# Seven PSUM banks in one pool, a bank named for each fill, and norms' gains and shifts applied behind the transpose

## Chip, cores and metric

The kernel runs on one core of one Trainium2 chip. The metric is the device time of one execution in microseconds, the median of several. All data are float32.

## The reference

The input x has 32 sequences of 64 rows by 256 features, and ctx has the same shape. Five attention blocks follow each other, here by the letters of the kernel's stages:

- n, a and d (first layer): x is normalised over a whole sequence, with a gain and a shift by row. Queries come from the normalised x, keys and values from ctx; 8 heads of 64 channels attend over the 256 feature positions, softmax(q k) v, then an output projection, a bias and x added.
- k and b (second layer): a = layernorm(ctx)*g + b; keys and values a @ Wk, a @ Wv; 16 heads of 16 over 64 keys; x + tanh(gate) * out.
- k and e (third layer): queries from x, keys and values from ctx and x together (128 keys), output projection and residual; then rmsnorm with a gain, `gelu(out @ w1 + b1) @ w2 + b2`, residual.
- c (fourth layer, first half): layernorm(x)*s1 + b1, self-attention with a mask, residual.
- k and f (fourth layer, second half): layernorm(x)*s2 + b2, attention over ctx, residual; layernorm(x)*s3 + b3, a gelu MLP, residual. The result is the output.

## The kernel before, in words

**Tiling.** Two sequences are one pair (128 rows), so there are 16 pairs. Each pair passes through the stages n, a, d, k, b, e, c, f. Every stage is written once for each engine as a Python generator (`pe_a`, `act_a`, `dve_a`, `pool_a` and so on); each `yield` ends a step.

**Order.** `weave` (called at the end of `build` for each engine) takes the strings of `ORDER`, one letter a step, and issues the steps of all pairs in that order. The order of work on every engine is thus fixed by these strings, and an engine that waits holds back all that is behind it on that engine. The strings of TensorE let stage a of later pairs run between b, e, c and f of earlier ones.

**Setup (stage s).** Before the pairs, gains and shifts of the norms are folded into weights: 80 matmuls with one column (L1135) multiply the weights by the norms' shifts, giving `fold` (used as biases), then VectorE multiplies eight weight blocks by the gains (L1196) and one by tanh(gate) (L1200), and four pairs of matmuls (L1146) turn value biases into rows, `row_bias`. The first transpose of stage d waits for `row_bias` (`setup["row"]`), and so do the projections of stage k (`ready`).

**Banks.** PSUM has eight banks of 512 columns here. Before the change four have fixed users in stages a and d: two for the scores and for the projections of queries and keys (`scores_bank`), one for transposed probabilities (`transposed_bank`), one for the attended values (`attended_bank`). All other stages share four (`banks`), taken in turn: `fill_places` gives fill number k the bank k % 4. `fill_bank` waits until the last reader of the bank's last fill has released it, `filled` says that it is full, `wait_fill` waits for that, `release` gives it back and `written` waits for the release.

**Stages a and d.** Of a pair there are 8 units (two sequences n, four pairs of heads j). `project(j)` (L441) fills both score banks, ScalarE and VectorE copy them out with a bias as q_a and k_a. `score` (L452) fills both banks with scores of two heads, and waits for the exponentials of the unit before. VectorE takes the maxima (L488), ScalarE the exponentials with their sums (L524), VectorE the reciprocals (L494), GpSimd multiplies (L538). `transpose` (L555) then fills `transposed_bank` for e = 0, waits for ScalarE's copy (L602, `pt0`), fills it for e = 1, and the next unit waits for VectorE's copy (L588, `pt1`). `attend` (L570) multiplies by the values.

**Norms of k, e, c, f.** VectorE computes statistics and the normalised rows, GpSimd the power -1/2, TensorE transposes (L607) and `act_copy` (L804) copies the transpose out in one 128x256 instruction; gains and shifts are in the weights already. ScalarE also runs Exp and Gelu; between the two a table is loaded.

**Residuals.** `pool_residual` (L764) adds a row of `row_bias` to the residual on GpSimd in every attention; in stage b that is a row made of the folded value bias.

## Time and profile before

| | us |
|---|---|
| median of 3 runs | 1444.21 (1443.49 to 1444.38) |
| the profiled execution | 1449.69 |
| its span, first to last instruction | 1447.9 |
| TensorE busy (matmul) | 1331.4 |
| VectorE, ScalarE, GpSimd busy | 1062.8, 812.6, 784.5 |
| mean granted TensorE clock | 0.963 |

The profiled execution is the one that all rows come from; the span is what its rows cover, and its own time is 1.8 us longer. A busy time counts instructions of that engine; the rest of the span is idle time, most of it waiting for another engine.

### The profile page before, as it was taken

The numbers are of one execution on the slowest core, as the hardware profiler recorded it, in microseconds if no ns is written. First come the engines' busy times: TensorE is split into PE (matmuls) and PEld (weight loads), VectorE is DVE, ScalarE is ACT, GpSimd is POOL, SyncE is SP. The second block draws the span as 40 slices with busy tenths as digits, with TensorE's granted clock in tenths as the row PEclk, the third lists the DMA queues.
The fourth block names the chain that finished last, engine by engine and source line by source line (L and its number), as shares of the span: only waits on it lengthen the run. The fifth ranks groups of instructions, "written<-read, shape, count | busy, mean of one in ns | idle before, by whom it ended". The sixth has DMA issues, their size and how long they took to land. (4 is left out here: it accounts for less than half of the span.)

```text
span 1447.9 us, 33972 instructions
## 1 busy us (share of the span) xinstructions
PE 1331.4 (92%) x12752; PEld 990.0 (68%) x12752; DVE 1062.8 (73%) x2251; ACT 812.6 (56%) x2043; POOL 784.5 (54%) x1072
## 2 busy tenths in 40 slices
PE   5898999999999999999999899999999999989685
PEld 4665666768686676867677676868686775757564
DVE  3458796887877878787877869697868778675742
ACT  2155557557575666665565656566566656654332
POOL 1145365565665665565565657474655656563631
PEclk8599999999999999999999999999999999999896
DMA  8000000000000000000000000000000000000000
GB/s 324 14 9 12 17 2 5 22 5 17 6 21 6 20 7 15 8 10 17 6 21 6 20 7 16 11 6 17 6 21 6 9 18 1 2 6 5 1 5 4
DMA packets 22815, 26.49 MB, mean 18 GB/s; under 512 B 9600, under 2 KB 21888, under 8 KB 22400
## 3 DMA queue, kind: packets, MB, share of 16 engines
q1 hardware_dynamic: 22656, 24.33, 5.2%
q8 instruction: 105, 1.72, 0.5%
q14 instruction: 54, 0.44, 0.1%
HBM read 22.22 MB, written 2.10 MB: 17 GB/s over the span
## 5 line engine op out<-in xcount | busy, mean ns | idle before, releaser
L538 POOL TENSOR_SCALAR p_a<-p_a,rec_a 128x256 f32<-128x256 f32 x512 | 249.4, 506 | 184.3 <-DVE rec_a L494 184.2
L524 ACT ACTIVATE p_a<-scores,nmax_a 128x256 f32<-128x256 f32 x512 | 236.3, 474 | 101.5 <-DVE nmax_a L488 96.8
L488 DVE TENSOR_REDUCE nmax_a<-scores 128x2 f32<-128x512 f32 x256 | 165.5, 680 | 50.4 <-PE scores L452 49.1
L555 PE MATMUL transposed<-ident,p_a 128*128 128x128 f32 x1024 | 166.1, 286 | 27.6 <-DVE p_a L588 9.8
L555 PEld LDWEIGHTS transposed<-ident,p_a 128*128 128x128 f32 x1024 | 114.4, 143 | 90.5 <-issue 62.6
L452 PE MATMUL scores<-k_a,q_a 64*128 64x256 f32 x1024 | 149.8, 412 | 7.0 <-ACT p_a L524 2.8
L570 PE MATMUL attended<-p_a,v_a 128*64 128x256 f32 x1024 | 134.9, 393 | 2.7 <-DVE p_a L588 2.6
L452 PEld LDWEIGHTS scores<-k_a,q_a 64*128 64x128 f32 x1024 | 92.8, 191 | 40.7 <-issue 27.5
L602 ACT ACTIVATE p_a<-transposed 128x512 f32<-128x512 f32 x128 | 76.8, 600 | 74.1 <-PE transposed L555 73.8
L524 ACT ACTIVATION_READ_ACCUMULATOR p_a<-scores,nmax_a 128x1 f32 x512 | 105.1, 205 | 0.0
L570 PEld LDWEIGHTS attended<-p_a,v_a 128*64 128x64 f32 x1024 | 65.0, 138 | 51.6 <-issue 19.8
L588 DVE COPY p_a<-transposed 128x512 f32<-128x512 f32 x128 | 86.7, 677 | 14.5 <-PE transposed L555 14.3
L740 POOL TENSOR_TENSOR e_kblk<-e_kT,row_mask 128x512 f32<-128x512 f32 x64 | 67.2, 1070 | 40.1 <-DVE e_kT L829 23.6
L441 PE MATMUL scores<-xc,wqk 64*128 64x512 f32 x256 | 75.1, 663 | 10.2 <-ACT p_a L524 7.5
L755 POOL TENSOR_TENSOR e_p<-e_p,e_rec 128x1024 f32<-128x1024 f32 x32 | 60.9, 1907 | 41.2 <-DVE e_rec L705 41.1
L508 ACT ACTIVATE q_a<-scores,bqk 128x512 f32<-128x512 f32 x64 | 43.9, 687 | 40.3 <-PE scores L441 40.1
L841 PE MATMUL bank<-f_xnT,wc 128*128 128x128 f32 x512 | 64.4, 281 | 1.0 <-ACT f_xnT L804 0.9
L475 DVE TENSOR_SCALAR k_a<-scores,bqk 128x512 f32<-128x512 f32 x64 | 47.4, 740 | 23.5 <-PE scores L441 23.2
L841 PE MATMUL bank<-e_qT,wb 128*128 128x128 f32 x512 | 63.9, 281 | 0.5 <-ACT e_qT L804 0.5
L841 PEld LDWEIGHTS bank<-f_xnT,wc 128*128 128x128 f32 x512 | 60.9, 196 | 4.4 <-ACT f_xnT L804 2.5
L841 PEld LDWEIGHTS bank<-e_qT,wb 128*128 128x128 f32 x512 | 60.6, 195 | 4.0 <-issue 2.0
L850 PE MATMUL bank<-wc,f_p 128*128 128x256 f32 x256 | 62.1, 388 | 0.0
(253 smaller groups left out, 3146.3 us busy)
## 6 DMA issues: line engine op xcount, KB each, us to landing
wb<-in_wb SPq DMA_DIRECT2D x1, 4096.0 KB, 14.8
wc<-in_wc SPq DMA_DIRECT2D x1, 4096.0 KB, 25.3
xc<-in_x SPq DMA_DIRECT2D x16, 128.0 KB, 2.6
xc<-in_ctx SPq DMA_DIRECT2D x16, 128.0 KB, 2.8
c_top<-in_ctx SPq DMA_DIRECT2D x16, 128.0 KB, 2.7
k_c<-in_ctx SPq DMA_DIRECT2D x16, 128.0 KB, 2.0
res_a<-in_x SPq DMA_DIRECT2D x16, 128.0 KB, 2.0
out<-y_out SPq DMA_DIRECT2D x16, 128.0 KB, 1.7
```

The source lines that it names most:

```text
L441: last = mm(ps[:, :], wqk[rows_, 2 * j:2 * j + 2, :], xc[rows_, z, :, :], start=True, stop=True)
L452: ins = mm(scores_bank[e][:, qt * D:(qt + 1) * D], q_a[rows_, j % 2, n, qt * P:(qt + 1) * P], k_a[rows_, j % 2, n, :], start=True, stop=True)
L488: dve.tensor_reduce(nmax_a[:, n, e, :], scores_bank[e][:, :].rearrange("p (q k) -> p q k", q=KT), AX.X, ALU.max, negate=True).then_inc(A.s ...
L524: last = act.activation(p_a[:, j % 2, n, e, qt, :], scores_bank[e][:, qt * D:(qt + 1) * D], ACT.Exp, bias=nmax_a[:, n, e, qt:qt + 1], accu ...
L538: last = pool.tensor_scalar(p_a[:, j % 2, n, e, qt, :], p_a[:, j % 2, n, e, qt, :], rec_a[:, n, e, qt:qt + 1], 1.0, ALU.mult, ALU.mult)
L555: last = nc.tensor.transpose(transposed_bank[:, kt * D + qt * P:kt * D + (qt + 1) * P], p_a[:, j % 2, n, e, qt, kt * P:(kt + 1) * P], iden ...
L570: last = mm(attended_bank[n * S:(n + 1) * S, 0:D], v_a[:, n, kt, h * S:(h + 1) * S], p_a[:, j % 2, n, e, kt, :], start=h == 0 and kt == 0, ...
L588: dve.tensor_copy(p_a[:, j % 2, n, 1, :, :], transposed_bank[:, :].rearrange("p (k q) -> p k q", k=KT)).then_inc(A.s["pt1"], 1)
L602: act.activation(p_a[:, j % 2, n, 0, :, :], transposed_bank[:, :].rearrange("p (k q) -> p k q", k=KT), ACT.Copy).then_inc(A.s["pt0"], 1)
L740: pool.tensor_tensor(T.kblk[:, f, c, :, :, :], bc(keys, 2, HR), bc(bc(row_mask[:, :], 2, S), 1, 2), ALU.mult).then_inc(T.s[kblk], 1)
L841: last = mm(ps[:, m * P:(m + 1) * P], W["w1"][:, k, cols_], T.xnT[:, k, :], start=k == 0, stop=k == KT - 1)
L850: last = mm(ps[:, 0:D], T.hid[:, m, :], W["w2"][:, m, :], start=m == 0, stop=m == MT - 1)
```

## The change

Four things change. (1) Seven banks form one pool; only the bank of the attended values stays apart. Projections and scores of stage a, transposes of stage d and the setup's products are fills like all others, and the string `BANK` names a bank for each of the 1,637 fills. Waits for the counters `exp`, `pt0`, `pt1` and so on become waits for the release of the named bank. (2) Gains and shifts leave the weights: `act_scale` copies the transposed norm out in two 128x128 activations with a scale and a shift for each partition, in stages k, e, c and f (five norms a pair; that of e has no shift). The 80 fold matmuls and the eight scalings of weights are gone; three row products remain. (3) Stage b adds x1 itself, without `pool_residual`, and frees x1 only once its sum is written. (4) All order strings are new: stage n now comes ahead of the setup, and the transposes of the first pair no longer wait for `row_bias`; the queue on SyncE loads the first pair before the raw weights, and two raw weights go straight to their tile, half as many bytes. The query's factor S**-0.5 moves into the activation that copies queries out.

```diff
 UNITS = H0
-BANKS = 4
+BANKS = 7
...
+def score_fills():
+    fills = [(("qk", j, 0), ("qk", j, 1)) for j in range(2)]
+    for u, j, n in units():
+        fills.append((("s", u, 0), ("s", u, 1)))
+        if n and j + 2 < H0 // 2:
+            fills.append((("qk", j + 2, 0), ("qk", j + 2, 1)))
+    return tuple(fills)
+
+
...
 ORDER = {
...
     "pe": (
-        "snnnnaaassaaasssssankksssasnadkdkkdkddddkkkdadddddakdkdaddddadadadddabdnbadbadndaddddbbnabndakbddeaeeeadeedkad"
...
+        "nnsnnaaaaaaddaadddddaadddsskddkddaaknsddkddnddddkdkakaaadknnkbddakbabakaddndddaabbdddbnkddkaabddeddeeeeaeddddd"
...
+BANK = (
+    "012345601234560123456012364540512364035645103265416501634250163245016324560215340612540362514501652430243120436512"
...
-    return {fill: (k % BANKS, k // BANKS) for k, fill in enumerate(fills)}
+    assert len(fills) == len(BANK)
+    used = [0] * BANKS
+    places = {}
+    for fill, b in zip(fills, map(int, BANK)):
+        places[fill] = b, used[b]
+        used[b] += 1
+    return places
 
...
+        def place(T, i, name):
+            return places["d" if T is A and name[0] == "x" else T.name, i, name]
+
...
-                        pe.wait_ge(setup["wvo"], 3)
+                        pe.wait_ge(setup["raw_in"], 64)
                     pe.wait_ge(N.s["norm"], N.at(i, "norm", 2))
                     pe.wait_ge(N.s["c_in"], N.at(i, "c_in", 32))
-                    if i:
-                        pe.wait_ge(A.s["exp"], A.at(i, "exp", 0))
-                elif j == 1:
-                    pe.wait_ge(A.s["q_sb"], A.at(i, "q_sb", 1))
-                    pe.wait_ge(A.s["k_sb"], A.at(i, "k_sb", 1))
-                else:
-                    pe.wait_ge(A.s["exp"], A.at(i, "exp", 4 * (j - 1)))
-                for rows_, ps in zip((slice(0, S), slice(S, P)), scores_bank):
-                    last = mm(ps[:, :], wqk[rows_, 2 * j:2 * j + 2, :], xc[rows_, z, :, :], start=True, stop=True)
-                last.then_inc(A.s["qk_ps"], 1)
+                for half, rows_ in enumerate((slice(0, S), slice(S, P))):
+                    ps = fill_bank(A, pe, i, ("qk", j, half))
+                    filled(A, mm(ps[:, :], wqk[rows_, 2 * j:2 * j + 2, :], xc[rows_, z, :, :], start=True, stop=True), i, ("qk", j, half))
 
             def score(u, j, n):
-                ready = min(j + 2, H0 // 2)
-                pe.wait_ge(A.s["q_sb"], A.at(i, "q_sb", ready))
-                pe.wait_ge(A.s["k_sb"], A.at(i, "k_sb", ready))
-                if u:
-                    pe.wait_ge(A.s["exp"], A.at(i, "exp", 2 * u))
+                written(A, pe, i, ("qk", j, 0))
+                written(A, pe, i, ("qk", j, 1))
+                if i or j > 1:
+                    pe.wait_ge(A.s["att"], A.at(i, "att", 2 * (j - 1)))
+                bs = [fill_bank(A, pe, i, ("s", u, e)) for e in range(2)]
                 for qt in range(KT):
                     for e, rows_ in enumerate((slice(0, S), slice(S, P))):
-                        ins = mm(scores_bank[e][:, qt * D:(qt + 1) * D], q_a[rows_, j % 2, n, qt * P:(qt + 1) * P], k_a[rows_, j % 2, n, :],
+                        ins = mm(bs[e][:, qt * D:(qt + 1) * D], q_a[rows_, j % 2, n, qt * P:(qt + 1) * P], k_a[rows_, j % 2, n, :],
                                  start=True, stop=True)
                         if qt == KT - 1:
-                            ins.then_inc(A.s["scores"], 1)
+                            filled(A, ins, i, ("s", u, e))
...
                 pe.wait_ge(A.s["prob"], A.at(i, "prob", 2 * u + e + 1))
-                if e:
-                    pe.wait_ge(A.s["pt0"], A.at(i, "pt0", u + 1))
-                elif u or i:
-                    pe.wait_ge(A.s["pt1"], A.at(i, "pt1", u))
-                else:
-                    pe.wait_ge(setup["consts"], IDENT)
-                    pe.wait_ge(setup["row"], 1)
+                ps = fill_bank(A, pe, i, ("x", u, e))
                 for qt in range(KT):
                     for kt in range(KT):
-                        last = nc.tensor.transpose(transposed_bank[:, kt * D + qt * P:kt * D + (qt + 1) * P],
+                        last = nc.tensor.transpose(ps[:, kt * D + qt * P:kt * D + (qt + 1) * P],
                                                    p_a[:, j % 2, n, e, qt, kt * P:(kt + 1) * P], ident[:, :])
-                last.then_inc(A.s["trans"], 1)
+                filled(A, last, i, ("x", u, e))
...
-            dve.wait_ge(T.s["res"], T.at(i, "res", 1))
+            if T is B:
+                dve.wait_ge(A.s["x1"], A.at(i, "x1", 1))
+                residual = x1[:, i % AHEAD, :]
+            else:
+                dve.wait_ge(T.s["res"], T.at(i, "res", 1))
+                residual = T.res[:, 0, :]
             ps = wait_fill(T, dve, i, "p")
-            release(T, dve.tensor_tensor(dst, ps[:, 0:D], T.res[:, 0, :], ALU.add), i, "p")
+            release(T, dve.tensor_tensor(dst, ps[:, 0:D], residual, ALU.add), i, "p")
...
+        def act_scale(T, i, name, gain, shift):
+
+            act = nc.scalar
+            yield
+            if i == 0:
+                act.wait_ge(setup["cols_in"], 32)
+            ps = wait_fill(T, act, i, name)
+            for k in range(KT):
+                more = {"bias": col(shift)[:, k:k + 1]} if shift else {}
+                last = act.activation(T.xnT[:, k, :], ps[:, k * P:(k + 1) * P], ACT.Identity, scale=col(gain)[:, k:k + 1], **more)
+            release(T, last, i, name)
...
-            yield from act_copy(K, i, "nT", K.xnT[:, :, :])
+            yield from act_scale(K, i, "nT", "l1_g", "l1_b")
...
-            yield from pool_residual(B, i, 0, x1[:, i % AHEAD, :], 0, lambda pool: pool.wait_ge(A.s["x1"], A.at(i, "x1", 1)), "p")
...
-            yield from act_copy(F, i, "nT0", F.xnT[:, :, :])
+            yield from act_scale(F, i, "nT0", "l3_g2", "l3_b2n")
             yield from act_attention(F, i)
-            yield from act_copy(F, i, "nT1", F.xnT[:, :, :])
+            yield from act_scale(F, i, "nT1", "l3_g3", "l3_b3n")
...
+            for n, wo in enumerate((WBt["o1"], WCt["o0"], WCt["o1"])):
+                yield
+                pe.wait_ge(setup["spread"], 3)
+                arrived(pe, 0)
+                ps = fill_bank(X, pe, 0, ("row", n + 1))
                 for k in range(KT):
-                    last = mm(ps[:, (n // 2) * D:(n // 2 + 1) * D], spread[:, n, k, :], W[name][:, k, :],
-                              start=k == 0, stop=k == KT - 1)
-                last.then_inc(setup["row_ps"], 1)
-
-        row_banks = [transposed_bank, attended_bank]
+                    last = mm(ps[:, 0:D], spread[:, n, k, :], wo[:, k, :], start=k == 0, stop=k == KT - 1)
+                filled(X, last, 0, ("row", n + 1))
...
-            for dst, src in ((wv_raw[:, :, :], dram["wv0"]), (wo_raw[:, :, :], dram["wo0"]), (wq_raw[:, :, :], dram["wq0"]),
-                             (wk_raw[:, :, :], dram["wk0"])):
+            for dst, src in ((wv_raw[:, :, :], dram["wv0"]), (wo_raw[:, :, :], dram["wo0"]),
+                             (wqk[0:S, :, :], dram["wq0"][0:S, :].rearrange("p (h c) -> p h c", c=P)[:, :, 0:S]),
+                             (wqk[S:P, :, :], dram["wk0"][S:P, :].rearrange("p (h c) -> p h c", c=P)[:, :, 0:S])):
```

## Rows read from the trace of the kernel before

**Rows 1.** The page: the span, and busy time of each engine (its share, instructions).
```profile
span 1447.9 us, 33972 instructions
PE 1331.4 (92%) x12752; PEld 990.0 (68%) x12752; DVE 1062.8 (73%) x2251; ACT 812.6 (56%) x2043; POOL 784.5 (54%) x1072
```

**Rows 2.** Windows: stretch, length, busy time (instructions) by engine, granted clock, DMA share, GB/s.
```profile
0.00:106.00 106.00, 81.49 (x484) 59.67 (x486) 45.77 (x131) 32.30 (x100) 27.51 (x60) 0.81 0.33 117
106.00:1340.00 1234.00, 1177.74 (x11612) 873.98 (x11612) 963.84 (x2019) 747.49 (x1888) 715.35 (x973) 0.99 0.04 11
1340.00:1448.00 108.00, 72.20 (x662) 56.36 (x658) 53.21 (x102) 32.86 (x56) 41.69 (x41) 0.81 0.01 3
```

**Rows 3.** Timeline of TensorE, 0 to 106 us: start, duration, instructions [idle before, releaser].
```profile
9.86 3.67 PE L1117 MATMUL scores<-p_a 64*128 64x64 f32 x16 [9.86 <-DMA p_a<-in_wk]
...
27.42 3.57 PE L1135 MATMUL transposed<-cols,wb 128*128 128x1 f32 x16
...
40.73 13.81 PE L1135 MATMUL transposed<-cols,wc 128*128 128x1 f32 x64
...
62.29 2.04 PE L1146 MATMUL transposed<-wb,e_p 128*128 128x256 f32 x4 [4.40 <-DVE wb L1200]
...
68.65 1.13 PE L1146 MATMUL attended<-wc,e_p 128*128 128x256 f32 x4
...
104.48 1.08 PE L570 MATMUL attended<-p_a,v_a 128*64 128x256 f32 x8 [0.34 <-DVE p_a L588]
```

**Rows 4.** Windows: a stretch of the setup.
```profile
27.00:67.00 40.00, 31.96 (x129) 26.20 (x126) 17.11 (x57) 9.27 (x36) 8.00 (x17) 0.50 0.24 79
```

**Rows 5.** Timeline, TensorE and GpSimd: the first unit's scores, and its probabilities.
```profile
25.93 1.57 PE L452 MATMUL scores<-k_a,q_a 64*128 64x256 f32 x8 [0.94 <-DVE k_a L475]
...
30.52 1.84 POOL L538 TENSOR_SCALAR p_a<-p_a,rec_a 128x256 f32<-128x256 f32 x4 [11.98 <-DVE rec_a L494]
```

**Rows 6.** Timeline of TensorE at the full clock: one step of each kind.
```profile
80.28 1.06 PE L614 MATMUL bank<-k_cT,wc 128*128 128x128 f32 x8
...
82.30 0.44 PE L607 MATMUL bank<-ident,k_c 128*128 128x128 f32 x2
...
83.10 1.14 PE L452 MATMUL scores<-k_a,q_a 64*128 64x256 f32 x8
```

**Rows 7.** Waits of TensorE, 106 to 1340 us: total, times, longest.
```profile
PE transposed L555 <- DVE p_a L588: 9.8, 11, 2.0
PE transposed L555 <- POOL p_a L538: 8.7, 6, 3.5
PE transposed L555 <- ACT p_a L602: 7.0, 9, 1.5
PE scores L441 <- ACT p_a L524: 4.8, 6, 2.0
...
PE scores L452 <- ACT p_a L524: 2.8, 8, 0.9
...
PE attended L570 <- DVE p_a L588: 2.0, 5, 0.6
```

**Rows 8.** Groups of ScalarE: count, busy us, mean ns, idle before.
```profile
L867 ACT ACT_TABLE_LOAD x37 | 47.5, 1283 | 0.7
...
L716 ACT ACT_TABLE_LOAD x25 | 32.1, 1283 | 0.5
...
L524 ACT ACT_TABLE_LOAD x11 | 14.1, 1283 | 0.2
...
L804 ACT ACTIVATE k_xnT<-bank 128x256 f32<-128x256 f32 x16 | 6.1, 383 | 2.3 <-PE bank L607 2.3
```

**Rows 9.** The page: the exponentials on ScalarE, one activation with a bias by partition.
```profile
L524 ACT ACTIVATE p_a<-scores,nmax_a 128x256 f32<-128x256 f32 x512 | 236.3, 474 | 101.5 <-DVE nmax_a L488 96.8
```

**Rows 10.** Groups of GpSimd, 108 to 1340 us: stage b's residual.
```profile
L764 POOL TENSOR_TENSOR b_res<-x,row_bias 128x256 f32<-128x256 f32 x15 | 11.6, 773 | 1.7 <-DVE x L595 1.5
```

**Rows 11.** The chain that ended last: start, duration, what.
```profile
1413.76 0.39 ACT f_xnT L804
```

More of the change, by code:

```diff
@@ L53, in attention_fills, with units, transpose_fills @@
             + tuple((("t", r, c),) for r in range(KT) for c in range(blocks)) + (("o",), ("p",)))
+def units():
+    return [(2 * j + n, j, n) for j in range(H0 // 2) for n in range(2)]
+def score_fills():
[5 more added lines that the diff above has]
+    return tuple(fills)
+def transpose_fills():
+    fills = []
+    for u, j, n in units():
+        fills += [(("x", u, e),) for e in range(2)]
+        if n:
+            fills += [(), ()]
+    return tuple(fills)
 FILLS = {
+    "s": (("wvo", "bias"), (("row", 1),), (("row", 2),), (("row", 3),)),
+    "a": score_fills(),
+    "d": transpose_fills(),
     "n": (("mean",), ("var",), (("v", 0, 0), ("v", 0, 1)), (("v", 1, 0), ("v", 1, 1))),
@@ L466, in pe_a, with scored, keys_free @@
                     project(j + 2)
+        def scored(eng, i, j):
+            for e in range(2):
+                wait_fill(A, eng, i, ("s", 2 * j + 1, e))
+        def keys_free(eng, i, j):
+            if j > 1:
+                scored(eng, i, j - 2)
+            elif i:
+                scored(eng, i - 1, j + 2)
         def dve_a(i):
@@ L670, in pe_attention @@
             written(T, pe, i, "o")
+            if i == 0 and T is B:
+                pe.wait_ge(setup["scaled"], 1)
             dst_free(pe)
@@ L1036, in act_c @@
         def act_c(i):
-            yield from act_copy(C, i, "nT0", C.xnT[:, :, :])
+            yield from act_scale(C, i, "nT0", "l3_g1", "l3_b1n")
             yield from act_values(C, i, "v", C, 0)
@@ L1138, in pe_s @@
-            last.then_inc(setup["fold_ps"], 1)
-            for n, (W, name) in enumerate(((WBt, "o0"), (WBt, "o1"), (WCt, "o0"), (WCt, "o1"))):
-                yield
-                pe.wait_ge(setup["spread"], 4)
-                pe.wait_ge(setup["scaled"], 9)
-                ps = row_banks[n % 2]
+                    last = mm(ps[half * S:(half + 1) * S, 0:1], wo_raw[:, h, :], bv_raw[:, h:h + 1], start=h == 0, stop=h == H0 - 1)
+            filled(X, last, 0, "bias")
+            for n, wo in enumerate((WBt["o1"], WCt["o0"], WCt["o1"])):
+                yield
+                pe.wait_ge(setup["spread"], 3)
+                arrived(pe, 0)
+                ps = fill_bank(X, pe, 0, ("row", n + 1))
```

334 lines of the change are left out of this document (163 added, 171 removed).

## Prediction

> **What bounds the kernel now.** I read the page first: TensorE is busy for 1331.4 us of a span of 1447.9, every other engine for less than three quarters [rows 1]. So TensorE is the bound, and time can only come from its idle time, 116.5 us, from work that it no longer does, or from its clock. The windows say where the idle time is [rows 2]: 24.5 us in the first 106 us (106 - 81.5), 56.3 in the 1234 us after it (4.6%), 35.8 in the last 108. The first stretch ends with the last product of pair 0's attended values, at 105.56 (the last row of [rows 3]). The timeline shows what TensorE does there: it waits 9.9 us for the raw weights, spends 17.4 us (3.57 + 13.81) on the one-column products of the fold, does four row products (the first and last of four lines, 2.04 and 1.13 us; 6.9 for the four) after waiting 4.4 us for VectorE's scaling of weights, and only then makes the first transpose [rows 3]. Between 27 and 67 us it runs at a granted clock of 0.50, the lower level, 1.2 GHz, although busy 32 of 40 us [rows 4]. The waits of the middle stretch are mostly those of stages a and d for their fixed banks [rows 7].
>
> **The sum.** It is made against the profiled execution, 1449.7 us, whose span is 1.8 shorter. The median of the runs shown, 1444.2, is 0.38% lower, so the end is scaled by 0.9962.
>
> **1. Setup and first pair.** Gone from TensorE: the fold, 17.4 us, and the wait for scaled weights, 4.4 [rows 3]. Of four row products three stay; at the full clock one takes 1.13 [rows 3], I take 4.0 for three, 2.9 less. Up to the same last product of pair 0 the new order string has one step of scores more (+1.14) and two projections (1.06 each) and two transposes of stage k (0.44 each) fewer [rows 6]: 1.9 us less here, and owed later. That makes 59.3 us of work (81.5 - 17.4 - 2.9 - 1.9). Of the idle time, 20.1 us remain (24.5 - 4.4), of which 9.9 is the transfer. But the fold covered part of pair 0's own chain. A unit takes 6.4 us from the start of its scores to its probabilities (25.93 to 32.36) [rows 5]; the new string puts the scores of the second unit, a projection and the scores of the third between, some 3.4 us, so the first transpose waits about 2 us. Later units have more between. I charge 3 us; the ends are 0 and 14 (the longer part of the fold, 13.81 us, covered waiting throughout). The lower clock costs the kept work some 4.4 us there: of 32.0 busy us between 27 and 67 [rows 4], 17.4 are the fold's and 5.8 the first three row products' (6.9 - 1.13) [rows 3], and 8.8 us of other work at half the clock are 4.4 at the full one. With less waiting and no one-column products I take 3 of them back; bounds 0 and 4.4, and a longer slow phase is a rival. The stretch becomes 59.3 + 20.1 + 3 - 3 = 79.4, that is 26.6 less, and with 1.9 owed 24.7.
>
> The arrival of the large weights does not hold this: stage k and the row products now wait for both weight tiles, but in the new string they stand behind 25 steps, about 26 us of work after 9.9, and the DMA share has fallen to 0.24 in the mean of 27 to 67 us [rows 4]; before, the row products needed them too. On SyncE's queue stage n's three transfers now stand ahead of the raw weights (384 KB), and the raw weights have 512 KB less: I count 0, bounds -1 and +2. VectorE's sixteen scalings go with the fold; they ran in the same gap and count nothing more.
>
> **2. Banks in the middle stretch.** Waits for a fixed bank's reader are 9.8 and 7.0 us for the transposes, 4.8 for the projections and 2.8 for scores, 24.4 in all [rows 7]. Two transposes of a unit now have two banks, and scores no longer need the bank of the unit before. I counted in the two TensorE strings how much TensorE work lies between the end of a bank's last fill and its next. For the transposes of stage d 146 of 255 had under 2.5 us, now 58; for the steps of scores and projections 37 of 191, now 12 fills of 384. I take the 24.4 as gone. Two waits are not for banks: 8.7 us for probabilities and 2.0 for the copied transposes [rows 7]. Between scores and the transpose of the same unit the new string leaves at least 7.4 us of work instead of 5.8, and 2.2 instead of 1.6 ahead of the second product of values; half of 10.7 goes, 5.4. Against that the other stages now share with a and d: fills with under 1.5 us rise from 32 to 58. I charge 3 us for them; bounds 0 and 25 (one microsecond each for the 26 more). The remaining 21 us of the middle's idle time stay. Sum: 26.8 less. What is late next is GpSimd's probabilities and the norms' chains, which have lengths of their own.
>
> **3. Gains and shifts on ScalarE.** A copy of 128x256 takes 383 ns [rows 8], an activation of the same size with a bias by partition 474 [rows 9]. Two halves with scale and bias cost between 383 and 948 ns, so 0 to 0.57 us more; I take 0.4, nearer the dearer row since both carry pointers. Eighty norms make 32 us of ScalarE. Counted in its two strings, though, the switches between Exp and Gelu fall from 74 to 52; a table load takes 1.283 us (37, 25 and 11 loads in three groups, 1.4 us idle before them in all) [rows 8], so 28 us go. ScalarE at 56% [rows 1] hides the difference. In the last pair nothing hides it: the chain that ends last runs through this copy [rows 11], with four such norms one after another (e, c and two of f), +1.6 us.
>
> The Trainium skill (ScalarE: Activation LUTs, What ACT_TABLE_LOAD costs) speaks against this edit: each operand that is a pointer adds about 93 ns to an activation. By its figures two halves take 865 ns and the copy 399, an estimate of 0.47 us more, 37 us of ScalarE and 1.9 at the end instead of 1.6. The same section puts a switch of tables at 2.66 us with a drain; the trace agrees on the load (1283 ns) and not on the drain, since almost no idle time stands before the loads [rows 8]. By the page 22 switches would be worth 59 us of ScalarE.
>
> **4. The rest.** Sixteen additions of stage b's residual leave GpSimd, 0.773 us each [rows 10], 12 us of an engine at 54% [rows 1]: 0 for the end. x1 is held until stage b's sum; four buffers rotate and the string has stage b of pair i-4 some 250 us of TensorE work ahead, so 0. The new wait of `score` for the attended values is for TensorE's own earlier instruction: 0. The step from a folded bias to a column or a copy on VectorE: 0. The tail of the string has the same work behind the last product of pair 15 (95 steps before, 93 now): 0, bounds -3 and +3.
>
> Total: 1449.7 - 24.7 - 26.8 + 1.6 = 1399.8, scaled 1394.5. I predict **1394 us**, 3.5% faster.
>
> **The rivals.** (A) *The banks move the waits and don't remove them*: the middle keeps its 56 us because the chain scores, maximum, exponential, probability sets the pace. For it: 8.7 us already wait for GpSimd. Against: the larger rows are waits for a bank. 1449.7 - 24.7 + 1.6 = 1426.6, scaled **1421**. (B) *More goes*: all of the 10.7, no new bank waits (3), no lost cover (3), the full clock early (1.4), and some 10 of the other 21 as the new strings leave more room: 22.7 less than forecast, **1372**. (C) *The first pair is bound by its chain at the lower clock*: the fold's cover is missed in full (11 more) and the slow phase lasts through the first pair (about 9 more): **1414**. For it: the clock fell in rows with gaps of 1 to 3 us between steps. (D) *Slower*: a named bank is a wait for one reader. In the whole new string 271 fills have under 2.5 us of TensorE work since their bank's last fill. A late reader on VectorE (73% busy) stalls TensorE even where another bank is empty, and everything behind it. At 0.3 us each that is 81 us instead of the 3: **1472**; from 0.19 us each it turns the sign. Against: before, 366 such fills cost some 25 us, 0.07 each. (E) *It doesn't do what it says*: the transposes of pair 0 still start late because ahead of them a raw weight or a column arrives late; the gain of step 1 falls to some 5 us, also near 1414, and I put it with C.
>
> **Chances.** Forecast 0.50, B 0.20, A 0.14, C with E 0.06, D 0.07, and 0.03 for two losses together that land at no change. Differences under about 0.2% can't be told from none here. Faster 0.90, same 0.03, slower 0.07. The range 1366 to 1422 holds the forecast with the bounds of its terms, A, B and C.
>
> **What would show it.** No one-column products; first transpose of stage d before 40 us instead of 72, last product of pair 0 near 79 instead of 105.6; TensorE busy near 1307; waits of L555 for the copies near nothing, of projections and scores too; total idle of the middle near 30 us; 52 table loads; activations of xnT of 128x128 at about 0.4 us. Wrong if TensorE waits in the middle sum to over 80 us, if its granted clock there falls below 0.97, or if stage k's or the row products' wait for weights opens a gap over 5 us.

## The result, and the profile after

The changed kernel takes 1382.99 us (median of 4, 1382.49 to 1384.94) against 1444.3 for the kernel before beside it (1443.49 to 1448.2): ratio 0.9568, 95% interval 0.9554 to 0.9582. The forecast was 1394, its range 1366 to 1422.

The page after, its rows on span and busy time; they answer to [rows 1].

```profile
span 1380.5 us, 34075 instructions
PE 1287.4 (93%) x12668; PEld 975.6 (71%) x12668; DVE 1049.5 (76%) x2226; ACT 808.0 (59%) x2101; POOL 770.8 (56%) x1056
```

The span fell by 67.4 us: TensorE is busy for 44.0 us less, and idle for 93.1 instead of 116.5. Windows of the changed kernel, cut as in [rows 2], at the last product of pair 0 and 108 us ahead of the end.

```profile
0.00:62.20 62.20, 50.85 (x380) 37.62 (x382) 37.82 (x103) 29.89 (x94) 27.05 (x58) 1.00 0.53 185
62.20:1272.50 1210.30, 1166.72 (x11678) 882.51 (x11674) 959.81 (x2023) 744.78 (x1951) 706.50 (x961) 1.00 0.04 11
1272.50:1380.50 108.00, 69.81 (x614) 55.45 (x614) 51.89 (x100) 33.33 (x58) 37.23 (x38) 0.81 0.01 3
```

The first stretch is 43 us shorter and the middle 24. The last cut is a fixed length and no event, so it can't show whether the end became longer. Cut at an event, the last product of stage d's values of pair 15, it did: first the kernel before, then the changed one.

```profile
1306.79:1447.90 141.11, 104.06 (x1018) 83.71 (x1018) 72.70 (x145) 48.56 (x85) 53.84 (x54) 0.85 0.01 4
1232.54:1380.50 147.96, 104.77 (x1011) 85.23 (x1010) 74.29 (x150) 52.24 (x95) 56.08 (x57) 0.86 0.01 4
```

Up to that product the middle is 30.9 us shorter; behind it, with as much work of TensorE's, the changed kernel needs 6.9 us more. The timeline of TensorE in the first stretch, against [rows 3]:

```profile
4.81 0.34 PE L390 MATMUL bank<-mv_a,mean_of_all 64*64 64x2 f32 x2 [4.81 <-DVE mv_a L417]
...
8.79 3.67 PE L1197 MATMUL bank<-p_a 64*128 64x64 f32 x16 [2.46 <-DMA wqk<-in_wk]
...
25.25 0.63 PE L601 MATMUL bank<-ident,p_a 128*128 128x128 f32 x4 [1.04 <-POOL p_a L588]
...
37.32 1.10 PE L1211 MATMUL bank<-wb,e_p 128*128 128x256 f32 x4
38.26 1.03 PE L1211 MATMUL bank<-wc,e_p 128*128 128x256 f32 x4
...
45.99 1.13 PE L1211 MATMUL bank<-wc,e_p 128*128 128x256 f32 x4
...
61.11 1.08 PE L617 MATMUL attended<-p_a,v_a 128*64 128x256 f32 x8
```

The first transpose stands at 25.25 us; the three row products find the large weights there; the last product of pair 0 ends at 62.19 instead of 105.56; and the granted clock is 1.00 (2.4 GHz) from its first record, at 18.3 us, to the end of the stretch, where before it was 0.50 (1.2 GHz) for 40 us [rows 4]. The trace has no record of the clock ahead of 18.3 us; the windows count such time as 1.00.

Waits of TensorE in the changed kernel's middle, 62.2 to 1272.5 us (total, times, longest), against [rows 7]:

```profile
PE bank L655 <- DVE f_yT L843: 4.8, 5, 2.1
PE bank L689 <- issue: 3.2, 6, 1.1
PE bank L662 <- ACT f_xnT L871: 2.7, 3, 0.9
PE bank L700 <- POOL f_p L811: 2.4, 4, 1.3
PE bank L601 <- ACT p_a L574: 1.8, 3, 1.2
PE attended L617 <- DVE p_a L635: 1.5, 3, 0.7
```

The transposes' 9.8 and 7.0 us for the copies and the projections' 4.8 are gone, and of the 8.7 for probabilities 1.4 are left. All waits of stages a and d for scores, projections, transposes and values (L441, L452, L555 and L570 before, L476, L486, L601 and L617 after) fell from 37.8 us to 9.8. Above them in the list stand the norms, keys and attention of the other stages, which had been lower in the list. In all the middle's idle time fell only from 56.3 to 43.6 us; the rest of its 24 us, 11.4, is less busy time (1178.1 to 1166.7, from the window that begins at 105.56 before).

Groups of ScalarE after (count, busy us, mean ns, idle before), against [rows 8]:

```profile
L939 ACT ACT_TABLE_LOAD x26 | 33.4, 1283 | 0.5
L871 ACT ACTIVATE f_xnT<-bank,cols 128x128 f32<-128x128 f32 x64 | 25.8, 458 | 22.6 <-PE bank L655 22.6
L771 ACT ACT_TABLE_LOAD x19 | 24.4, 1283 | 0.3
L871 ACT ACTIVATE e_qT<-bank,cols 128x128 f32<-128x128 f32 x32 | 10.1, 378 | 8.0 <-PE bank L655 8.0
L574 ACT ACT_TABLE_LOAD x6 | 7.7, 1283 | 5.5 <-PE bank L486 5.5
L455 ACT ACT_TABLE_LOAD x1 | 1.3, 1283 | 0.8 <-PEq L1412 0.8
```

That is 52 loads, as counted from the strings; a half with scale and bias takes 458 ns, one with a scale alone 378, the whole copy took 383 [rows 8]. The two halves of a norm overlap: 25.8 us for the 32 norms of stage f are 0.81 us a norm, and 10.1 us for the 16 of stage e are 0.63.

### The profile page after: what moved, and what is told of

Read it like the earlier page. It is cut to its first block and busy times, and to the rows that moved or that the text cites. A ratio compares the mean times of both kernels' runs of the same rounds, so it can differ in the third digit from the quotient of the medians.

```text
span 1380.5 us, 34075 instructions
## 1 busy us (share of the span) xinstructions
PE 1287.4 (93%) x12668; PEld 975.6 (71%) x12668; DVE 1049.5 (76%) x2226; ACT 808.0 (59%) x2101; POOL 770.8 (56%) x1056
## 5 line engine op out<-in xcount | busy, mean ns | idle before, releaser
L574 ACT ACTIVATE p_a<-bank,nmax_a 128x256 f32<-128x256 f32 x512 | 236.8, 476 | 91.3 <-DVE nmax_a L536 90.7
L536 DVE TENSOR_REDUCE nmax_a<-bank 128x2 f32<-128x512 f32 x256 | 166.9, 680 | 13.5 <-PE bank L486 13.2
L601 PE MATMUL bank<-ident,p_a 128*128 128x128 f32 x1024 | 144.7, 277 | 6.0 <-POOL p_a L588 2.7
L486 PE MATMUL bank<-k_a,q_a 64*128 64x256 f32 x1024 | 138.7, 396 | 2.9 <-ACT p_a L574 1.1
L617 PE MATMUL attended<-p_a,v_a 128*64 128x256 f32 x1024 | 133.9, 389 | 4.2 <-DVE p_a L635 1.6
L601 PEld LDWEIGHTS bank<-ident,p_a 128*128 128x128 f32 x1024 | 113.7, 141 | 33.6 <-issue 25.2
L486 PEld LDWEIGHTS bank<-k_a,q_a 64*128 64x128 f32 x1024 | 91.7, 186 | 32.9 <-issue 22.6
L574 ACT ACTIVATION_READ_ACCUMULATOR p_a<-bank,nmax_a 128x1 f32 x512 | 105.8, 207 | 0.0
L617 PEld LDWEIGHTS attended<-p_a,v_a 128*64 128x64 f32 x1024 | 65.4, 136 | 54.5 <-issue 27.9
L635 DVE COPY p_a<-bank 128x512 f32<-128x512 f32 x128 | 86.1, 679 | 14.7 <-PE bank L601 14.3
L650 ACT ACTIVATE p_a<-bank 128x512 f32<-128x512 f32 x128 | 76.9, 602 | 31.9 <-PE bank L601 31.6
L476 PE MATMUL bank<-xc,wqk 64*128 64x512 f32 x256 | 71.6, 636 | 0.0
```

What stands on the lines that cost most here:

```text
L476: filled(A, mm(ps[:, :], wqk[rows_, 2 * j:2 * j + 2, :], xc[rows_, z, :, :], start=True, stop=True), i, ("qk", j, half))
L486: ins = mm(bs[e][:, qt * D:(qt + 1) * D], q_a[rows_, j % 2, n, qt * P:(qt + 1) * P], k_a[rows_, j % 2, n, :], start=True, stop=True)
L536: dve.tensor_reduce(nmax_a[:, n, e, :], ps[:, :].rearrange("p (q k) -> p q k", q=KT), AX.X, ALU.max, negate=True).then_inc(A.s["max"], 1)
L574: last = act.activation(p_a[:, j % 2, n, e, qt, :], ps[:, qt * D:(qt + 1) * D], ACT.Exp, bias=nmax_a[:, n, e, qt:qt + 1], accum_out=sum_a[ ...
L601: last = nc.tensor.transpose(ps[:, kt * D + qt * P:kt * D + (qt + 1) * P], p_a[:, j % 2, n, e, qt, kt * P:(kt + 1) * P], ident[:, :])
L617: last = mm(attended_bank[n * S:(n + 1) * S, 0:D], v_a[:, n, kt, h * S:(h + 1) * S], p_a[:, j % 2, n, e, kt, :], start=h == 0 and kt == 0, ...
```

## The experiments

Spans are of the profiled runs; ratios are against the kernel before on the same chip, whose median was 1446.3 (e1 to e4), 1446.5 (e5 to e8) and 1446.6 (e9 to e11). By its ratio the changed kernel, 0.9568, would take 1383.8 to 1384.1 us there. "Behind" is behind the last product of pair 0.

**e4, the setup part alone.** The kernel before with the fold taken out and the halves on ScalarE, its four fixed banks, pool and strings kept (steps of the setup that are empty now keep their places). The main lines of the edit:

```diff
-            yield from act_copy(K, i, "nT", K.xnT[:, :, :])
+            yield from act_scale(K, i, "nT", "l1_g", "l1_b")
...
-                        last = mm(transposed_bank[:, at:at + 1], W[name][:, k, m * P:(m + 1) * P], col(beta)[:, k:k + 1],
-                                  start=k == 0, stop=k == KT - 1)
...
-                    last = dve.tensor_scalar(W[name][:, k, :], W[name][:, k, :], col(g)[:, k:k + 1], None, ALU.mult)
```

> The kernel before with the second part of the change alone: no fold products, no scaling of weights by gains, gains and shifts in two 128x128 activations behind each transposed norm. Banks and all order strings stay as before; the steps of the setup that are left empty keep their places. Theory: the setup part gives what leaves TensorE ahead of its first transpose (17.4 us of products and 4.4 of waiting for scaled weights), and one row product fewer, so 20 to 27 us less, 1417 to 1424; the rest of the 61 us are banks and order. Rival A (the copies in two halves and their latency cost as much as the fold gave, so that the part alone is worth little without new orders): over 1435. Rival B (the slow clock of the setup goes with the one-column products too): under 1412.

Measured: 1437.99 us (1436.94 to 1441.54), ratio 0.9948 (0.9932 to 0.9965), 8 us faster: the time that its rival A gave, not the theory's. The timeline of e4 puts the last product of pair 0 here:

```profile
85.01 1.08 PE L570 MATMUL attended<-p_a,v_a 128*64 128x256 f32 x8 [0.34 <-DVE p_a L588]
```

It ends at 86.1, 19.5 us earlier than before. Behind it the kernel needs 1349.4 us to the end of the span, where before needed 1342.3: 7 us are lost again in these two executions, and rather 11 by the medians, which differ by 8.3. Two things more stand in e4's windows:

```profile
28.10:45.20 17.10, 9.74 (x35) 5.81 (x36) 8.51 (x28) 5.73 (x22) 6.92 (x13) 0.50 0.46 149
0.00:86.10 86.10, 59.25 (x398) 39.88 (x398) 38.92 (x108) 32.88 (x102) 28.05 (x59) 0.90 0.40 144
```

The clock still falls, for 17.1 us, though the one-column products are gone; TensorE is busy for 9.7 of them. And TensorE's idle time up to that product is 26.9 us, where 20.1 would be left of the 24.5 before without the wait for scaled weights: in the old order the fold had covered 6.8 us of the first pair's own waits.

**e11, the same without the scaled halves**, to see whether those lose the 7 us:

```diff
-            for k in range(KT):
-                last = act.activation(T.xnT[:, k, :], ps[:, k * P:(k + 1) * P], ACT.Identity, scale=col(gain)[:, k:k + 1], **more)
+            last = act.activation(T.xnT[:, :, :], ps[:, 0:D].rearrange("p (k q) -> p k q", k=KT), ACT.Copy)
```

> e4 (the kernel before with the setup part alone) with each transposed norm copied by one plain 128x256 Copy, the gains and shifts left out of the result. e4 won 19.5 us up to the last product of the first pair and gave 7 us of it back behind it. Theory: the two scaled halves, 80 times 0.53 us longer on ScalarE, gave back most of the 7 us in an order made without them; e5 measured 4 to 6 us for them in the new order. So this run is 5 to 9 us below e4: 1429 to 1433. Rival: the loss is the early start itself (what the setup hid before is now waited for behind it), and this run stays within 2 us of e4, 1436 to 1440.

Measured: 1427.82 us (1426.19 to 1429.76), ratio 0.9880 (0.9859 to 0.9901). The span is 1425.1 against e4's 1435.5: the halves cost 10 us in the old order. The theory holds, with a little more than it asked: pair 0 ends at 86.1 as in e4, and behind it the kernel needs 1339.0 us instead of 1349.4.

**e5, the same edit to the changed kernel.**

> The changed kernel with each transposed norm copied by one 128x256 ScalarE Copy again, so the gains and shifts of the norms are left out of the result; banks and orders stay. It asks what the two scaled halves cost in the order that was made for them. By the traces a norm's ScalarE work gets some 0.53 us shorter (two halves of 0.46 us against 0.383 us), 80 times, 40 us of ScalarE in all. Theory: ScalarE has room and only the chain at the end feels it, so the time falls by 1 to 2 us against the changed kernel, to about 1381 to 1382. Rival: the halves stand in TensorE's path in the middle as well (TensorE waits 4.6 us for the ScalarE norm copies there), and may be what made the fold-less kernel of before lose 7 us behind its first pair: then 1374 to 1377.

Measured: 1378.86 us (1376.45 to 1380.76; a fifth execution took 4243 us and is left out, its cause isn't known), ratio 0.9527 (0.9513 to 0.9541). The span is 4.7 us shorter than the changed kernel's, the ratio 0.0041 lower, 5.9 us. It lies between theory and rival: the halves cost 4 to 6 us here, not the 1.6 of the forecast, and half of what they cost in the old order. The waits of e5's middle show one of the places (2.7 us in the changed kernel):

```profile
PE bank L662 <- ACT f_xnT L869: 1.4, 3, 0.5
```

**e3, the fold put back into the changed kernel**, its 80 one-column products in the bank of the first row product, with nothing reading them:

```diff
+                if n == 0:
+                    at = 0
...
+                        for m in range(blocks):
+                            for k in range(KT):
+                                mm(ps[:, at:at + 1], W[name][:, k, m * P:(m + 1) * P], col(beta)[:, k:k + 1], start=k == 0, stop=k == KT - 1)
+                            at += 1
```

> The changed kernel with the one-column products of the fold put back ahead of the first row product, written to its bank and overwritten (they serve nothing). Nothing waits for them but what stands behind them on TensorE. Theory: setup work on TensorE counts one for one, since TensorE is the bound from the first product on: at the full clock about 0.18 us a record, 80 records, 14 us more, about 1397; if the weak activity of one-column products lowers the granted clock as it was before, up to 25 us more. Rival: the first pair's chain on the other engines hides them: under 5 us more.

Measured: 1402.2 us (1400.18 to 1404.31), ratio 0.9697 (0.9682 to 0.9712); the span is 17.7 us longer. The timeline and the window of e3:

```profile
37.58 1.92 PE L1217 MATMUL bank<-cols,wb 128*128 128x1 f32 x16
39.35 10.70 PE L1217 MATMUL bank<-cols,wc 128*128 128x1 f32 x64
49.91 2.05 PE L1220 MATMUL bank<-wb,e_p 128*128 128x256 f32 x4
51.76 1.65 PE L1220 MATMUL bank<-wc,e_p 128*128 128x256 f32 x4
...
75.03 1.08 PE L617 MATMUL attended<-p_a,v_a 128*64 128x256 f32 x8
```

```profile
30.00:62.20 32.20, 31.64 (x215) 26.61 (x215) 15.34 (x41) 12.52 (x43) 9.36 (x19) 0.84 0.21 56
```

TensorE hardly waits there (31.64 of 32.20 us), and still the granted clock falls to 0.84 in the mean, in the stretch that holds the one-column products: it is 0.50 from 42.8 to 53.0 us; the row products behind them take 2.05 and 1.65 us instead of 1.10 and 1.03. The products themselves cost 12.3 us (37.58 to 49.91), the slower ones behind them 1.6. The last product of pair 0 is 13.9 us later, and 3.8 more come behind it. No wait is given back here: its whole length counts. But the fold stands behind the first transposes in e3, where TensorE has no waits for it to cover. What it covered in its old place is e4's to tell, 6.8 us.

**e1 and e2, TensorE's order alone.** TensorE's string of the changed kernel with some steps moved by up to three places, so that neighbouring steps have the same tile form more often (725 changes of form, counted from its rows) or less often (872); the changed kernel has 798, the one before 868. The form is the entry with a star in a MATMUL row (128\*128, 64\*128, 128\*64 and so on). In both traces, four transposes (L601) start-to-start took 0.44 us where the steps on both sides have the same form, 0.49 where the one ahead differs, 0.53 where the one behind does, 0.59 where both do. The names of the banks stay with their fills. The first line of TensorE's string that differs, of e1 and then of e2:

```diff
-        "nnsnnaaaaaaddaadddddaadddsskddkddaaknsddkddnddddkdkakaaadknnkbddakbabakaddndddaabbdddbnkddkaabddeddeeeeaeddddd"
+        "nnsnnaaaaaaddaadddddaadddsskddkddaaknsddkddnddddkdkakaaadknnkbddakbabakaddndddaabbdddbnkddkaabddeddeeeeaeedddddda"
+        "nnsnnaaaaaaddaadddddaadddsskddkddaaknsddkddnddddkdkakaaadknbnkddabakbakaddndddababdddbnkddkabaddeddeeeeadeddddad"
```

> The changed kernel with 125 places of TensorE's order string exchanged, each step moved by at most three places, so that neighbouring steps use the array in the same tile form (128x128, 64x128, 128x64, 64x64, 128x32) more often: 724 changes of form instead of 797. Same work, same bank for each fill. Theory S (a change of tile form costs TensorE about 0.10 us, read from both traces: four transposes take 0.44 us between steps of their own form and 0.59 between steps of another): 73 x 0.10 = 7 us less, about 1376, if the moved steps open no new waits. Rival W (the lower busy time of the changed kernel comes from waits that are hidden in the records; the order of forms costs nothing): within 2 us of 1383, or slower by what the moves open.

> The mirror of the run before: 141 places exchanged under the same limits, so that the form of the tile changes 871 times instead of 797. Theory S: 74 x 0.10 = 7 us more, about 1390, all of it in TensorE's busy time. Rival W: within 2 us of 1383; or both this and its mirror slower by the same, which would be the price of moving steps and not of forms.

Measured: e1 1408.74 us (1406.71 to 1409.21), ratio 0.9739 (0.9725 to 0.9752); e2 1422.28 (1419.99 to 1424.36), ratio 0.9837 (0.9821 to 0.9853). Both expectations fell: they are 25 and 38 us slower than the changed kernel. Only their difference is as expected: 13.5 us for 147 changes, 0.092 us each. Two waits of e1, then one of e2:

```profile
PE attended L617 <- DVE p_a L635: 9.9, 7, 3.7
PE bank L689 <- issue: 7.8, 8, 1.5
```

```profile
PE bank L700 <- ACT p_a L574: 5.2, 2, 3.5
```

In e1's middle TensorE is idle for 68.2 us instead of 43.6. The copied transposes cost 9.9 us where they cost 1.5: VectorE's string still has them where TensorE's old order wanted them, behind work for others. A move of at most three steps in one of five strings made for each other costs as much as the whole gain of the middle, or more. The other part of the loss is the clock: it is 0.50 for 21.9 us of e1's middle and 23.9 of e2's, 10.2 of the changed kernel's. Of e1 and e2 themselves, e2's TensorE is busy for 16 us more there (1184.8 against 1168.8) and idle for 4 less, so the changes of form act on the busy time, as theory S has it.

**e6, more table loads.** One line more in stage e's Gelu:

```diff
                 h = T.hid[:, half * MT // 2:(half + 1) * MT // 2, :]
+                if half and T is E:
+                    nc.scalar.activation(idle[:, :], gate[:, :], ACT.Exp)
```

> The changed kernel with a one-column Exp put ahead of the second Gelu half in stage e, so that ScalarE loads its table twice more for each of the 16 units: up to 32 loads of 1.28 us, 52 becoming 70 to 84. It asks whether the 22 loads that the change saves (74 to 52) are part of what it brings. Theory (ScalarE has room, 808 of 1380 us busy): not over 3 us slower than the changed kernel, 1383 to 1386. Rival: each load delays a product that TensorE waits for, and the time grows by half of them or more: 1398 to 1405; then the saved loads are worth some 10 to 15 us of the gain in the middle.

Measured: 1406.18 us (1405.53 to 1409.22), ratio 0.9721 (0.9708 to 0.9734), 22 us slower than the changed kernel. ScalarE's groups show 82 loads (41, 19, 15, 6, 1). The largest wait of TensorE in e6, 62 to 1272 us:

```profile
PE bank L923 <- ACT e_p L942: 12.1, 9, 2.6
```

The rival holds, a little above its range: 30 loads cost 22 us, 0.74 each, on an engine that is busy for 60% of the span. Most of TensorE's added idle time is at one place, the product behind that Gelu: 12.1 us where the changed kernel has 0.5, of some 16 more in the whole middle. It says what a load costs ahead of a product that is due, not what each of the 22 saved ones was worth where it stood.

**e7, all five orders and the banks' names anew.** ORDER and BANK are the only edits; the first lines of TensorE's string and of BANK:

```diff
-        "nnsnnaaaaaaddaadddddaadddsskddkddaaknsddkddnddddkdkakaaadknnkbddakbabakaddndddaabbdddbnkddkaabddeddeeeeaeddddd"
+        "nnsaaannaaddaadkdandddakddankddkddkdaddssakdddksaakdddaaddknnbadbabdddaddadadabbddbnddbdkeaneekdeeddaeddddakdkda"
-    "012345601234560123456012364540512364035645103265416501634250163245016324560215340612540362514501652430243120436512"
+        "3154620421463026145320165423501021345603414564213506520314124021432104234652410143052306046132546206102162054230"
```

> The changed kernel with the five engines' orders and the bank names written anew, from the changed kernel's own, by a search that moves single steps in all five orders together and renames single fills, counting about 0.09 us for each change of tile form in TensorE's order; 730 changes of form against 798, no other edit. It asks whether the limit of the order is reached, and whether e1 and e2 lost their time because only TensorE's order was moved. Theory: with the other engines' orders and the banks moved along, the 68 fewer form changes (6 us) and fewer waits come through: 1345, between 1335 and 1365. Rival: a step away from the given order costs whatever moves with it, as in e1 and e2: 1390 to 1420.

Measured: 1382.53 us (1380.65 to 1384.12), ratio 0.9556 (0.9543 to 0.9569): level with the changed kernel, so neither expectation. The longest wait of e7 in its first 75 us:

```profile
PE bank L601 <- issue: 13.6, 1, 13.6
```

Before its first transpose at 39.5 us TensorE stands still for 13.6 us. The row of TensorE names no releaser, but VectorE's timeline shows the cause:

```profile
37.45 0.43 DVE L826 BATCH_NORM_STATS2 k_stats<-k_c 128x6 f32<-128x256 f32 x1 [13.98 <-DMA k_c<-in_ctx]
```

e7's order of VectorE has the statistics of stage k ahead of pair 0's reciprocals and maxima, and stands for 14.0 us until k_c has landed; ScalarE, GpSimd and TensorE wait behind it.

**e8, the same search with the banks in three groups.** Again ORDER and BANK alone:

```diff
-    "012345601234560123456012364540512364035645103265416501634250163245016324560215340612540362514501652430243120436512"
+        "6510101034102532103521025610210450126321025210532421025102012012420126501625301232530145104260125621026465232016"
```

> The same search under one more rule: scores and projections of stage a only in banks 0 and 1, its transposes only in bank 2, all other fills in banks 3 to 6, the split that the kernel before had (within its groups the names stay free); the setup is the changed kernel's. 784 changes of form. Against e7 it prices the one pool by itself, each with orders made for it. Theory: the pool is worth what the middle of the trace showed, so this run is 22 to 35 us slower than e7. Rival: the new order, not the pool, did it, and this run comes within 8 us of e7.

Measured: 1422.18 us (1419.95 to 1423.43), ratio 0.9826 (0.9813 to 0.9839). By the medians e8 is 40 us slower than e7 (39 by the ratios, 41 by the spans). Waits of e8's middle:

```profile
PE bank L601 <- DVE p_a L635: 5.2, 9, 1.0
...
PE bank L486 <- DVE k_a L519: 4.4, 8, 1.4
...
PE bank L486 <- ACT p_a L574: 3.6, 13, 0.4
PE bank L601 <- ACT p_a L650: 3.5, 9, 0.6
```

The waits for the transposes' copies and for k_a are back. Both starts are poor, each with an order of its own (pair 0 ends at 79.5 us in e7, at 81.9 in e8), so that the difference lies behind them: 1337.8 us against 1298.9, TensorE idle for 19 more and busy for 20 more. The split costs more than the range expected; that the search did equally well under both rules is assumed, not shown.

**e9 and e10, with the start kept.** The strings begin as the changed kernel's and part behind the first pair; TensorE's first line in e9:

```diff
-        "nnsnnaaaaaaddaadddddaadddsskddkddaaknsddkddnddddkdkakaaadknnkbddakbabakaddndddaabbdddbnkddkaabddeddeeeeaeddddd"
+        "nnsnnaaaaaaddaadddddaadddsskddkddaaknsddkddnddddkdkakaaadnaddnbabdbkkkdadddaadddkndbbabdnbaeddedeeeadedkdaaddddk"
```

> As e7, but every engine's steps up to 62 us, and the banks of their fills, stay the changed kernel's; only what comes behind the first pair is ordered anew, 716 changes of tile form. e7 ended level with the changed kernel, and its trace shows 13.6 us of one TensorE wait ahead of the first transposes that the changed kernel does not have, with less idle time behind it. Theory: e7 lost at its start what it won behind it, so this run is 10 to 18 us below the changed kernel: 1366 to 1374. Rival: e7's start only hid time that is owed anyway, and it ends level again: 1380 to 1386.

> As e9, from another course of the search, one that asked the order to hold under three sets of scattered durations instead of two; 745 changes of tile form. Theory: form changes cost about 0.09 us each here too, so it ends 1 to 6 us behind e9. Rival: an order that bears scatter better is worth more than 29 form changes (2.7 us), and it ends ahead of e9.

Measured: e9 1367.04 us (1363.92 to 1369.78), ratio 0.9457 (0.9435 to 0.9478); e10 1371.44 (1369.5 to 1374.27), ratio 0.9489 (0.9470 to 0.9508). Both theories hold, the one on e10 weakly, as its interval meets e9's. Windows of e9:

```profile
0.00:62.20 62.20, 50.69 (x376) 37.30 (x376) 37.48 (x102) 29.70 (x93) 27.05 (x58) 1.00 0.53 185
62.20:1265.00 1202.80, 1157.16 (x11690) 883.28 (x11690) 986.91 (x2030) 763.61 (x1964) 714.58 (x965) 1.00 0.04 11
1265.00:1366.00 101.00, 69.65 (x610) 55.87 (x604) 48.27 (x95) 36.33 (x61) 32.85 (x33) 0.81 0.02 5
```

ScalarE loads its table 66 times in e9, not 52. The start is the changed kernel's to 0.2 us of busy time; behind it TensorE is busy 9.7 us less (1226.8 against 1236.5) and idle 5 us less. e9 is the fastest version here: 1.2% below the changed kernel by the two ratios (0.9457 and 0.9568), 5.4% below the one before.

## Why the prediction was right, step by step

The sum took 49.9 us off the profiled execution. The profiled ones differ by 67.2 (1449.69 to 1382.49), the medians by 61.3. The signs and the main mechanisms held: work and waits gone from the first pair, waits for fixed banks gone from the middle. The first term was too small, the second came out near by errors that cancel, the cost of the halves was read too low for the end, and the tail is longer than its bounds allow.

The runs split the 61 us thus: the setup edit alone 8 (e4), new strings for all engines under the old split of the banks, with stage b's residual, some 16 more (e8 against e4), one pool 40 more (e7 against e8; e7 is level with the changed kernel). The last two hang on the search having done equally well each time. No run has the new strings with the fold kept where it was, or stage b's residual (part 3) by itself.

**Step 1, setup and first pair (forecast -26.6 in the stretch, measured -43.4): the right parts, too small.** The prediction kept 20.1 us of idle time and charged 3 us for lost cover. The stretch holds 11.4 us of idle time in all (62.2 - 50.85), of which 8.1 stand ahead of the raw weights' first product, at 8.79 us. The term that was mis-sized is "20.1 us remain": nearly 9 of them went too, and the 3 for cover with them. In the old strings the lost cover was real, and larger than charged (6.8 us, e4); the new strings have other work there, and the first transpose waits 1.0 us, not 2. The work itself is 50.9 us where 56.3 was forecast: the clock after 18.3 us came back in full (4.4 us by the prediction's own bound, not 3), the three row products take 3.3 us and not 4.0, and the rest isn't split here. That the clock would rise because the one-column products go is only part of it: without them, in the old order, it still fell for 17.1 us (e4). The setup edit alone moved that product by 19.5 us, and the end by 8. The other 24 of the 43.4 come with the new strings and banks. The prediction had put the whole stretch down to the setup, and called "the banks move the waits" alone worth 1421; the setup alone is 1438.

**Step 2, the banks (forecast -26.8, -24.9 with what was owed; measured -24.0, or -30.9 up to pair 15's last product): near, by luck.** The waits of a and d fell by 28.0 us, 29.8 were forecast (24.4 and 5.4). The step that failed is "I charge 3 us" for the other stages, "the remaining 21 us of the middle's idle time stay": theirs rose by about 15 us, and idle time fell by 12.7. What filled the gap was not in the sum: TensorE's busy time fell by 11.4 us, though the stretch has 64 matmuls more (part of what was owed). Two amounts cover this. The middle has 749 changes of tile form instead of 801; 52 fewer are about 5 us at the 0.092 of e1 and e2. And the clock was at 0.50 for 23.9 us of the middle before, in six places (at 146, 211, 221, 303, 1122 and 1300 us), and for 10.2 us after, in two (at 257 and 1227), as here, one of each:

```profile
1299.70:1306.40 6.70, 5.26 (x24) 3.15 (x24) 3.81 (x8) 1.63 (x3) 3.36 (x5) 0.50 0.00 0
257.30:263.90 6.60, 5.72 (x34) 4.39 (x34) 4.63 (x10) 3.99 (x15) 5.45 (x6) 0.50 0.07 20
```

13.7 us less at half the clock are up to 6.9 us of work, an estimate. The prediction had no term for the clock behind the first pair; why it fell in each of these places stays open. e8 against e7 puts the pool at 40 us, so a split of the banks costs more than the waits for them in [rows 7] show: an order fitted to few banks is bent around them, and its other waits and form changes (784 against 730) belong to the price. Rival A is refuted by that, and rival D: no named bank shows a stall that sums up.

**Step 3, ScalarE (forecast +1.6): ScalarE's own time right, its worth wrong.** Two overlapping halves take 0.81 us where the copy took 0.38, so a norm with a shift costs 0.42 us more and one without 0.25: 31 us in all, as forecast (0.4 each, 32). The 0.53 us and 40 us in the expectations of e5 and e11 add the means of rows that overlap. "ScalarE at 56% hides the difference" is the sentence that failed: the halves cost 4 to 6 us in the new order and 10 in the old one (e5, e11). What the 22 saved table loads were worth is not measured. A load costs 0.74 us of the end where a product is due behind it (e6); but e9 is the fastest kernel here with 66 loads, so not every load costs that. A mean share says nothing of that: what counts is whether TensorE's next step is behind the instruction.

The forecast weighed a figure of a page against its 0.4. The Trainium skill (ScalarE: Activation LUTs, What ACT_TABLE_LOAD costs) has 93 ns for each pointer operand and 186 ns + 0.833 ns a column for an activation without. For a half that makes 479 ns with two pointers and 386 with one, estimates by the page; the rows have 458 and 378. For a norm the forecast's 0.4 us was a little nearer to the 0.42 measured than the 0.47 by the page.

**Step 4, the rest (forecast 0, the tail between -3 and +3): the tail was wrong.** Behind the last product of stage d's values of pair 15 the changed kernel needs 148.0 us, the one before 141.1, with 43.2 us idle instead of 37.1. The halves in the chain at the end make 1.7 of the 6.9 us (four times 0.42), as forecast under step 3; what makes the other 5 stays open. The late norms, residuals and probabilities are the chain, as they were.

Of the signs named ahead, the first transpose, the 52 loads, the waits of the transposes and the weights' arrival came as written. The last product of pair 0 (62 instead of 79), TensorE's busy time (1287 instead of 1307) and the middle's idle time (44 instead of 30) did not. Of rival B, at 1372, half came: all the lost cover, the full clock and more of the first pair's idle time, but new waits of other stages instead of 10 us fewer. 1383 lies midway between it and the forecast.

## What to carry to other kernels

With an order written out for each engine, an edit is worth what it is worth in an order made for it: the same setup edit gave 8 us under the old strings, and three-place moves in one string cost 25 to 38. Price a bank or a slot by what the order could do with it, not by the waits in the trace, since the order was already bent to avoid them. And before calling an engine's work hidden by its mean share, look at whether the bounding engine's next step stands behind it.

## What the runs showed of the hardware

- **A change of tile form between neighbouring TensorE steps costs about 0.09 us of the end, and up to 0.15 us of TensorE's time.** e1 and e2 differ by 147 changes and 13.5 us. In the rows, a change behind four transposes adds 0.09 us and one ahead of them 0.06, so the two sides of one change can make 0.15. The Trainium skill (TensorEngine Tiling (Array Packing), Key Properties) says that switching the tiling mode drains TensorE, without a price; by these runs the 798 changes of the changed kernel are some 70 us of its end, an estimate. Four transposes of the changed kernel between steps of their own form (L700 and L662; 0.43 us to the start of L662), then between two of other forms (L476 and L689; 0.59 to the start of L689):

```profile
178.81 0.60 PE L601 MATMUL bank<-ident,p_a 128*128 128x128 f32 x4
179.24 1.06 PE L662 MATMUL bank<-b_xT,wb 128*128 128x128 f32 x8
...
242.61 0.66 PE L601 MATMUL bank<-ident,p_a 128*128 128x128 f32 x4
243.20 1.09 PE L689 MATMUL bank<-e_kblk,e_qT 64*64 64x256 f32 x16
```

- **TensorE's first products run at half speed, and the windows don't show it.** Value products (L405) start 0.43 us apart up to 17.8 us, and 0.22 apart at 63 us. The first record of the clock is at 18.3 us; ahead of it a window gives 1.00 for want of one. In e8, with long waits at its start, the first record is at 40.4 us, and the same products are 0.43 us apart at 38 and 0.22 at 44:

```profile
16.49 0.63 PE L405 MATMUL bank<-wvo,c_top 64*128 64x256 f32 x1
...
16.92 0.63 PE L405 MATMUL bank<-wvo,c_top 64*128 64x256 f32 x1
...
63.53 0.38 PE L405 MATMUL bank<-wvo,c_top 64*128 64x256 f32 x1
...
63.75 0.38 PE L405 MATMUL bank<-wvo,c_top 64*128 64x256 f32 x1
```

- **The granted clock fell among one-column products while TensorE never rested**: 0.50 from 42.8 to 53.0 us in e3, 1.00 there in the changed kernel without them; the mean clock of all four executions of e3 is 0.972 to 0.975, that of the changed kernel's 0.979 to 0.981. It also fell without such products, where TensorE waited (e4). e3's row:

```profile
42.80:53.00 10.20, 10.20 (x42) 9.61 (x42) 0.42 (x1) 0.00 (x0) 0.00 (x0) 0.50 0.02 4
```
